# Mixture-of-experts stage: four-block super blocks with stationary weights, streamed rows and a raw-weight ring

## The reference

```python
logits = x @ gate_weight.T                       # 4096 tokens, E = 64 experts
top_val, top_idx = lax.top_k(softmax(logits), 8) # 8 experts for each token
...                                              # secondary picks may be remapped
order = jnp.argsort(flat_e); tok = order // 8
xs = x[tok]                                      # 32768 routed rows, sorted by expert
gu = lax.ragged_dot(xs, swap(gate_up_proj), group_sizes)   # 1024 -> 2 x 384
gate, up = jnp.split(gu, 2, axis=-1)
hact = jax.nn.silu(gate) * up
y = lax.ragged_dot(hact, swap(down_proj), group_sizes)     # 384 -> 1024
out = jnp.zeros_like(x).at[tok].add(y * w[:, None])        # weighted scatter-add
```

## Time and profile before

| what | value |
|---|---|
| runs | 8266.21, 8266.89 and 8268.61 us, median 8266.89 us |
| profiled execution, span from first to last instruction | 8265.9 us |
| PE busy in the span | 7509.6 us, 91% |
| first matmul of the expert stage | 3801.4 us |
| expert stage from there to the end | 4464.5 us, 54% of the span |
| blocks of the expert stage | 287 (64 of them the first of an expert) |

### The profile page before, as it was taken

How to read it: one execution, slowest core, us unless ns; L and a number is a source line. 1 busy time by engine, 2 the same in 40 slices (tenths; PEclk the granted TensorE clock), 3 DMA queues, 4 the chain that set the end, 5 groups by cost and what they waited for, 6 DMA issues and landing times.

```text
span 8265.9 us, 154435 instructions
## 1 busy us (share of the span) xinstructions
PE 7509.6 (91%) x49303; PEld 6709.6 (81%) x49304; DVE 4437.6 (54%) x9784; ACT 3440.3 (42%) x7330; POOL 1747.3 (21%) x1447
## 2 busy tenths in 40 slices
PE   8988998998996899866999999999999999999999
PEld 7877877887885777756888888888888888888888
DVE  6666666666664434455555555555454554555444
ACT  5665665665663212102333333333333333333333
POOL 1111111111110000002222233222222332333222
PEclk9999999999998999978999999999999999999999
DMA  1101101101102221114555555555555555555544
GB/s 56 32 24 49 31 24 49 32 24 49 32 24 75 72 83 61 64 46 119 139 139 137 138 139 138 139 137 138 134 142 126 143 145 126 142 145 139 131 126 115
DMA packets 419950, 786.53 MB, mean 95 GB/s; under 512 B 31120, under 2 KB 295312, under 8 KB 419600
## 3 DMA queue, kind: packets, MB, share of 16 engines
q0 software_dynamic: 89328, 328.81, 18.6%
q1 hardware_dynamic: 330272, 453.35, 16.9%
HBM read 578.60 MB, written 203.46 MB: 95 GB/s over the span
## 4 chain that ended last, share of the span: by engine, by line
PE 38%; issue 7%; POOL 6%; ACT 3%; ACTq 1%; DVE 0%; POOLq 0%; DMA 0%; DVEq 0%
PE ps_gu L1546 8%; PE ps_gu L1548 8%; PE ps_gu L1547 8%; POOL dn_lo L1530 4%; PE ps_y L1546 4%; PE ps_y L1547 3%; PE ps_y L1548 3%; PE ps_xe L1565 2%; ACT gu_hi L1662 2%; PE ps_h L1599 1%; POOL out L1524 1%; ACT y_out L1651 1%; ACTq L1459 1%; ACT xe_hi L1640 0%; DVE at_lo L1726 0%
## 5 line engine op out<-in xcount | busy, mean ns | idle before, releaser
L1546 PE MATMUL ps_gu<-gu_hi,xe_hi 128*128 128x256 f32 x6888 | 1983.3, 288 | 62.5 <-DVE gu_lo L1794 58.2
L1548 PE MATMUL ps_gu<-gu_hi,xe_lo 128*128 128x256 f32 x6888 | 1949.6, 283 | 0.0
L1547 PE MATMUL ps_gu<-gu_lo,xe_hi 128*128 128x256 f32 x6888 | 1949.2, 283 | 0.0
L1546 PEld LDWEIGHTS ps_gu<-gu_hi,xe_hi 128*128 128x128 f32 x6888 | 1323.5, 192 | 115.1 <-DVE gu_lo L1794 85.2
L1547 PEld LDWEIGHTS ps_gu<-gu_lo,xe_hi 128*128 128x128 f32 x6888 | 1321.5, 192 | 7.8
L1548 PEld LDWEIGHTS ps_gu<-gu_hi,xe_lo 128*128 128x128 f32 x6888 | 1320.1, 192 | 0.0
L1805 DVE TENSOR_TENSOR act_h<-ps_gu,silu 128x128 f32<-128x128 f32 x861 | 248.1, 288 | 1824.9 <-ACT silu L1673 1824.9
L1673 ACT ACTIVATE silu<-ps_gu 128x128 f32<-128x128 f32 x861 | 238.9, 277 | 1685.5 <-PE ps_gu L1548 1678.8
L1546 PE MATMUL ps_y<-dn_hi,ht_hi 128*128 128x512 f32 x1722 | 724.2, 421 | 108.5 <-POOL dn_lo L1530 108.5
L345 PE MATMUL ps_qkv<-w_hi,xt_hi 128*128 128x384 f32 x1920 | 708.7, 369 | 52.0 <-DVE v L635 51.9
L1524 POOL DMA_INDIRECT out<-y_out,scatter_i x287 | 516.4, 1799 | 1011.6 <-ACT y_out L1651 974.6
(11 more groups left out here) (273 smaller groups left out, 15357.6 us busy)
## 6 DMA issues: line engine op xcount, KB each, us to landing
gu_raw<-w_gu SPq DMA_DIRECT2D x192, 1024.0 KB, 10.3
dn_raw<-w_down SPq DMA_DIRECT2D x192, 512.0 KB, 4.8
w_raw<-wqkv SPq DMA_DIRECT2D x260, 192.0 KB, 2.6
out<-residual SPq DMA_DIRECT2D x33, 512.0 KB, 2.6
probs<-x SPq DMA_DIRECT2D x32, 512.0 KB, 3.5
attn_out<-out_t POOLq DMA_DIRECT2D x128, 128.0 KB, 2.2
residual<-x SPq DMA_DIRECT2D x32, 512.0 KB, 4.4
stage<-attn_out SPq DMA_DIRECT2D x32, 512.0 KB, 5.2
```

The source lines that it names most:

```text
L1546: pe.matmul(out, a_hi, w_hi, start=first, stop=False)
L1547: pe.matmul(out, a_hi, w_lo, start=False, stop=False)
L1548: return pe.matmul(out, a_lo, w_hi, start=False, stop=last)
```

## The change

An expert now has one unbranched super block of 4 x 128 = 512 rows (`SUP = 4`) and, in an inner loop, tail blocks of 128 rows for what it has beyond 512. With the given inputs these are 64 super blocks and 287 - 256 = 31 tail blocks, since every expert had at least four blocks; where an expert has fewer than 512 rows, the super block is filled up with spare rows of zeros.

In the super block's first layer a 128x128 piece of the weights is stationary and 512 columns of turned rows (`xs_hi`, `xs_lo`) stream; gate and up are products of their own. The result has the hidden features on the partitions, so silu(gate)*up is split in place into `hs_hi`, `hs_lo` without a transpose, and its 128-column slices are the stationary operand of the second layer (`weigh`), whose streamed operand is 512 columns of the down weights as before. Tail blocks are computed as blocks were before. The rows of the next expert's super block are gathered by four indirect transfers and turned between the parts of the second layer. The result of row block i goes to one of two buffers `y_sup[i % 2]`, that of the last one to `y_last`, by way of which tail blocks go too.

Raw weights come in nine chunks of 512 KB through a ring of three slots, with 4 KB in one piece for each partition where there were rows of 1 KB. All six `dn_lo` pieces are POOL's. 512 spare rows of `rows` and `out` are zeroed ahead of `mix_features` instead of 128.

The diff, cut to its core (PE, SP and POOL first, then ACT, then DVE):

```diff
+SUP = 4
+PAD = SUP * P
...
-            sp.dma_start(rows[0:P, 0:H], res[:, 0, :]).then_inc(zero_out, 16)
-            sp.dma_start(rows[0:P, H:H + E], res[:, 0, 0:E]).then_inc(zero_out, 16)
-            sp.dma_start(out[0:P, :], res[:, 0, :]).then_inc(zero_out, 16)
+            for i in range(SUP):
+                a = slice(i * P, (i + 1) * P)
+                sp.dma_start(rows[a, 0:H], res[:, 0, :]).then_inc(zero_out, 16)
+                sp.dma_start(rows[a, H:H + E], res[:, 0, 0:E]).then_inc(zero_out, 16)
+                sp.dma_start(out[a, :], res[:, 0, :]).then_inc(zero_out, 16)
...
-            after(dve.tensor_scalar(blocks[:, :], count[:, :], 1.0, None, ALU.max))
+            after(dve.tensor_scalar(blocks[:, :], count[:, :], float(SUP), 0.0, ALU.subtract, ALU.max))
...
+    HALF = HB * W // 2
+    GUC, CHUNKS = 2 * FB, 3 * FB
+    RING = 3
...
+                t0 = tails_before(eng, e)
+                t1 = tails_before(eng, e + 1)
+                super_block(e, t0, t1)
+                with eng.If(t1 - t0 > 0):
+                    with eng.Fori(t0, t1) as t:
+                        tail_block(e, t)
...
+                if c < GUC:
+                    src = w_gu[e, c // 2, :, c % 2 * HALF:(c % 2 + 1) * HALF]
...
+                    src = w_down[e, (c - GUC) * P:(c - GUC + 1) * P, :]
...
+            def slot_free(e, c):
+                if c < GUC:
+                    sp.wait_ge(lo_ok, START + e * 2 * GUC + 2 * (c + 1))
+                else:
+                    sp.wait_ge(dn_lo_ok, START + e * 2 * FB + 2 * (c - GUC + 1))
...
+                for c in range(RING, CHUNKS):
+                    slot_free(e - 1, c - RING)
+                    load(e - 1, c)
+                for c in range(RING):
+                    slot_free(e - 1, CHUNKS - RING + c)
                     load(e, c)
...
+                pool.wait_ge(ys_ok, START + e * 2 * (SUP - 1) + 2 * i + 2)
+                if i == 0:
+                    pool.wait_ge(ss_ok, START + e + 1)
+                    pool.wait_ge(yl_sent, LOADED + (e + t0 + 1) * 16)
                 stand_alone(pool, passed)
...
+                pool.indirect_dma_start(out, bass.IndirectOffsetOnAxis(ap=scatter_s[:, i:i + 1], axis=0), y_sup[:, i % 2, :], None,
+                                        compute_op=ALU.add).then_inc(ys_sent[i % 2], 16)
...
+            def super_block(e, t0, t1):
+                send_last(e + t0)
+                gather_tail(e + t0)
+                for i in range(SUP):
+                    gather_super(e + 1, i)
+                for n in range(2 * FB):
+                    pool.wait_ge(hi_ok, START + e * 2 * CHUNKS + 2 * GUC + n + 1)
+                    f, a = n // 2, slice(n % 2 * BANK, (n % 2 + 1) * BANK)
+                    pool.tensor_tensor(dn_lo[:, f, a], raw_w[:, f, a], raw(dn_hi[:, f, a]), ALU.subtract).then_inc(dn_lo_ok, 1)
+                for i in range(SUP - 1):
+                    send_super(e, t0, i)
...
+            def turn_super(n, i, tails):
+                pe.wait_ge(rows_s[i], (n + 1) * 16)
+                pe.wait_ge(xt_lo_ok, START + tails * 2)
+                pe.wait_ge(xs_lo_ok, START + n * 2 * SUP + 2 * i)
...
+                    for k in range(HB):
...
+                            pe.wait_ge(lo_ok, START + e * 2 * GUC + 4 * f + k // 2 + 1)
+                        c = slice(k * W + up * P, k * W + up * P + P)
+                        mm = split_product(ps_gu[:, up, :], gu_hi[:, f, c], gu_lo[:, f, c], xs_hi[:, k, :], xs_lo[:, k, :], k == 0, k == HB - 1)
+                    mm.then_inc(up_ok if up else gate_ok, 1)
...
+                    if i == 0:
+                        pe.wait_ge(hs_lo_ok, START + e * FB + f + 1)
+                        pe.wait_ge(dn_lo_ok, START + e * 2 * FB + 2 * f + c + 1)
...
+                    elif f == 0:
+                        pe.wait_ge(ys_ok, START + e * 2 * (SUP - 1) + 2 * (i - 1) + c + 1)
...
+                first_layer(0, 0)
+                first_layer(0, 1)
+                find_rows(e + AHEAD)
+                first_layer(1, 0)
+                first_layer(1, 1)
+                turn_tail(e + t0, e + 1)
+                first_layer(2, 0)
+                first_layer(2, 1)
+                turn_super(e + 1, 0, e + 1 + t0)
+                for f in range(FB - 1):
+                    for c in range(2):
+                        weigh(0, c, f)
+                for c in range(2):
+                    weigh(0, c, FB - 1)
+                for i in range(1, SUP):
+                    turn_super(e + 1, i, e + 1 + t0)
+                    for c in range(2):
+                        for f in range(FB):
+                            weigh(i, c, f)
...
+            def super_block(e, t0, t1):
+                def split(c):
+                    act.wait_ge(raw_in[c % RING], START + (e * 3 + c // RING) * 16 + 16)
+                    if c < GUC:
+                        act.wait_ge(up_ok, START + e * FB)
+                        act.wait_ge(tgu_ok, START + t0 * FB)
+                        dst = gu_hi[:, c // 2, c % 2 * HALF:(c % 2 + 1) * HALF]
...
+                    act.wait_ge(hs_lo_ok, START + e * FB + f)
+                    act.activation(act_s[:, :], ps_gu[:, 0, :], ACT.Silu).then_inc(silu_ok, 1)
...
+                    act.wait_ge(prod_ok, START + e * FB + f + 1)
+                    act.wait_ge(yl_ps, START + (e + t0) * 2 + 2)
+                    act.activation(hs_hi[:, f, :], act_s[:, :], ACT.Copy).then_inc(hs_hi_ok, 1)
...
+                    act.wait_ge(ys_sent[i % 2], LOADED + (e * (2 if i % 2 == 0 else 1) + i // 2) * 16)
+                    for c in range(2):
+                        act.wait_ge(ys_ps, START + e * 2 * (SUP - 1) + 2 * i + c + 1)
+                        a = slice(c * BANK, (c + 1) * BANK)
+                        act.activation(y_sup[:, i % 2, a], ps_y[:, a], ACT.Copy, scale=w_now[:, i:i + 1]).then_inc(ys_ok, 1)
...
+                act.activation(warm[:, :], warm[:, :], ACT.Silu)
+                split(0)
+                split(1)
+                finish_last(e + t0)
+                split(2)
+                split(3)
                 silu_of(0)
-                if first:
-                    split("gu", 2)
+                split_h(0)
+                split(4)
+                split(5)
+                silu_of(1)
+                split_h(1)
+                for c in range(GUC, CHUNKS):
+                    split(c)
+                split_tail(e + t0, t0)
+                silu_of(2)
+                split_h(2)
+                for i in range(SUP):
+                    split_super(e + 1, i)
+                    if i < SUP - 1:
+                        finish(i)
...
+                rest_of(0)
+                rest_of(1)
...
+                gather_tail_index(e + t0, (e + 1) * SUP + t0)
+                gather_super_index(e + 1, t1)
+                rest_of(2)
+                rest_of(3)
...
                 multiply(0)
-                if first:
-                    rest_of(2)
+                rest_of_h(0)
+                rest_of(4)
+                rest_of(5)
+                start_list(after)
+                list_part(after, 0)
+                list_part(after, 1)
+                multiply(1)
+                rest_of_h(1)
+                finish_list(e + AHEAD)
+                keep_tail_weights(e + t0, e)
+                rest_of_tail(e + t0)
+                dve.wait_ge(yl_ok, START + (e + t0) * 2 + 2)
+                dve.wait_ge(wnow_ok, START + e + 1)
+                dve.tensor_copy(w_last[:, :], w_now[:, SUP - 1:SUP]).then_inc(wl_ok, 1)
+                dve.wait_ge(yl_sent, LOADED + (e + t0 + 1) * 16)
+                dve.wait_ge(ss_ok, START + e + 1)
+                dve.tensor_copy(scatter_l[:, :], scatter_s[:, SUP - 1:SUP]).then_inc(sl_ok, 1)
+                multiply(2)
+                rest_of_h(2)
+                for i in range(SUP):
+                    rest_of_super(e + 1, i)
+                    if i == 0:
+                        keep_weights(e + 1)
+                    elif i < SUP - 1:
+                        list_part(after, i + 1)
+                    else:
+                        end_list(after)
...
-        "w_gu": tidy(i["L0_ffn_gate_up_proj"].reshape(E, 2, FB, P, H).transpose(0, 2, 4, 1, 3).reshape(E, FB, H, 2 * P)),
+        "w_gu": tidy(i["L0_ffn_gate_up_proj"].reshape(E, 2, FB, P, HB, P).transpose(0, 2, 5, 4, 1, 3).reshape(E, FB, P, HB * 2 * P)),```

Two places in the order of the instructions. PE, where the first layer of a block goes over into the second, before (`ps_h` takes the transpose of h, `ps_xe` those of the next rows):

```order
L1547 MATMUL ps_gu<-gu_lo,xe_hi 128x256
L1548 MATMUL ps_gu<-gu_hi,xe_lo 128x256
L1596 REGISTER_ALU
L1599 MATMUL ps_h<-ident,act_h 128x128
L1561 ISA
L1563 ISA
L1565 MATMUL ps_xe<-ident,x_rows 128x128 x8
L1596 REGISTER_ALU
L1599 MATMUL ps_h<-ident,act_h 128x128
L1609 REGISTER_ALU
L1546 MATMUL ps_y<-dn_hi,ht_hi 128x512
```

(15 more changed lines are left out.)

482 lines of the change are left out of this document (258 added, 224 removed).

## The result

The changed kernel took 7976.39 us (median of 4 runs, 7973.0 to 7983.38), the kernel before 8266.77 on the same chip: ratio 0.9648, interval 0.9636 to 0.966. That is 290 us less; the forecast was 346. The measured 7976 lies in the likeliest case's own range, 56 us above its number.

A forecast was written before the change was run, and what follows sets the result against it. PE, busy for 91% of 8265.9 us, bounds the kernel. 3821.4 us before the expert stage plus 4099 (super blocks 3597, borders 27, tails 464, end 11) gave 7920 us; range 7865 to 8045.

The forecast's parts named there:

- the likeliest case: Whole kernel: the sum of PE's work and waits holds, 7920 us, own range 7870 to 7980, chance 0.66.
- start: First matmul of the expert stage: at 3821.4 us, from 3801.4 before plus 7 for zeroing and 13 for the opening.
- work: PE's stream in the super blocks: 56.2 us each, 3540.6 us for 63 of them.
- end: Launch's end, last result scaled and scattered: the same 11 us as before; 67.2 with the last super block.
- The border, 0.8 us: Between super blocks of two experts: PE idle 0.8 us as before, under DVE's first remainder; 27 us in all.
- rival 1's third case: Border where ACT's table load comes in full behind DVE's work: 1.3 us; the rival gives 7985 to 8110, chance 0.17.
- Tails, 15.0 us: 31 tail blocks: 15.0 us for each of thirty ahead of a new expert, 14.3 for one, 464 in all.
- The super, 56.2 us: One super block on PE: triples 49.7, five turns of rows 5.2, list 0.99, restarts 0.3; before, four blocks cost 62.0.
- The rule against the row: First-layer matmuls: doubling width saves 0.010 us each, 1.5 us per expert by trace row; skill page gives 0.4 us.
- Waits: Inside a super block: weights, POOL's down remainders (2.2 us slack), last h part (0.5) and result buffers (3.6) stay hidden.
- Zeroing 7, opening 13: Ahead of the expert stage: nine more zeroing transfers cost 7 us, three more turns of rows with gathers 13.
- Rivals 3, 4, 5: Better than the sum, 7840 to 7865, 0.06; late sends, 8430, 0.04; few experts take the super block, excluded by counts.

The follow-up runs named there:

- Experiments 1 and 2: Changed kernel with DVE's value loads behind the first four remainders, 7896.32 us; changed kernel with DVE's list of rows one row block earlier, 7893.99 us.
- experiment 4: Changed kernel with the super block's first layer streaming its 512 columns as two matmuls of 256: 8045.06 us.
- Experiments 5: Kernel before with unused SBUF ahead of the stationary rows, 64 bytes for each partition or a large tile: 8174.04 and 8174.07 us.
- experiment 7: Changed kernel with late value loads, earlier list, tail gather before scatter, zeroing behind weights, plus 192 or 64 unused bytes ahead of xs_hi: 7828.24 and 7884.79 us.
- Experiment 3: Changed kernel with the tail's gather ahead of the scatter on POOL and the zeroing transfers behind the first weights on SP: 7933.48 us.
- experiment 8: Changed kernel with late value loads, earlier list, tail gather before scatter, and twelve zeroing transfers behind the first batch's context loads: 7841.82 us.
- experiment 9: Changed kernel with late value loads, earlier list, tail gather before scatter, zeroing behind context loads, and unused bytes at three places: 7811.03 us.

## Why the prediction was right, and by how much off

The mechanism was right: PE's stream is the bound, and four row blocks in one took out transposes, restarts and the waits inside. 7920 was 56 low. Against the profiled span of 7971.4 the terms were off by +2.7 (start), -56 (work), +73.5 (borders), +28 (tails) and +2.0 (end). That the sum came so near is luck in part: 102 us too few for borders and tails stood against 56 too many for the work of the supers.

- **The border, 0.8 us.** This term failed. I took 1.17 us of issue from the border of before, where only that much stood between DVE's work and its next cast. That issue held the same two value loads; here, behind the list, the first of them takes 1.32 in place of 0.3, and 2.54 us pass. The border was 2.4 us, 53 us more in all, and it brought 20 us of low clock, which the sum did not have. It is rival 1's third case (1.3 us for a late border) at half of the experts. Experiments 1 and 2 show the cause, and the clock's part. The sum had no low clock on either side: the window that it took for an expert of before stood at 1.00, and it did not count the 23 stretches elsewhere in that stage.
- **Tails, 15.0 us.** I took the tail from the last block of an expert before and held that row gathers cost nothing on PE, since they are issued early. That holds for the supers' gathers; I did not walk POOL's queue for the tail's, which stands behind the scatter of the last result: 0.9 us more in each of 31. Experiment 3 takes it out, and then the tail is 14.5, under the 15.0.
- **The super, 56.2 us.** It was 55.32. The medians of a first-layer triple are 0.69 as forecast. A turn of rows costs less than its own 1.04, since the next matmul starts ahead of its end: 0.79 by the starts, and 0.09 more until the one behind it (0.33 in place of 0.23). 5 x (1.04 - 0.88) = 0.8 is nearly the whole difference:

```profile
4190.90 1.04 PE L1632 MATMUL ps_xe<-ident,x_rows 128*128 128x128 f32 x8
4191.69 0.48 PE L1612 MATMUL ps_y<-dn_hi,hs_hi 128*128 128x512 f32 x1
4192.02 0.39 PE L1613 MATMUL ps_y<-dn_lo,hs_hi 128*128 128x512 f32 x1
```

- **The rule against the row.** The row said 0.010 us for each doubled matmul. The Trainium skill ("TensorE: Matmul & The Clock Gate", section "Back-to-back issue gap") gives a fixed part of 2.5 ns, in its formula for an isolated matmul. For the stream of this kernel experiment 4 measured 6 to 8 ns, between the two. Experiments 5 and 7 show that the row of before held a cost of the operands' place: at the offsets that were best for each, two of 256 took 0.228 to 0.234 and one of 512 took 0.227, so between 1 and 7 ns are left for the width. Part of the 1.5 us for each expert that I booked for it is placement. In time the change is worth 290 us against the kernel before as it stands, and some 198 against the same kernel with 64 unused bytes (medians of different chips), while the changed kernel had a place that cost it some 20 (experiment 7).
- **Waits.** PE had no wait on `dn_lo` or `hs_lo`, and none on the result buffers. POOL's remainder of 512 columns took 1.30 us at the mean (2.06 in the earlier trace rows), so its cover was never near its end:

```profile
L1591 POOL TENSOR_TENSOR dn_lo<-raw_w,dn_hi 128x512 fp32r<-128x512 f32 x384 | 485.2, 1298 | 1007.8 <-ACT dn_hi L1793 1007.8
```

- **Zeroing 7, opening 13.** Their sum of 20 was 2.7 short, but its parts do not stand as I had them. The first matmul of the mix stage came 7.4 us later after SP's first transfer than before, and by the stage's last gate matmul only 1.2 of them were left (3646.6 - 2524.5 against 3641.5 - 2520.6). The opening came to 17.6: 14.2 from the first turn of rows to the first matmul, for three turns more, and 3.4 ahead of it, from the last matmul of `route` on, where POOL was busy for 8.49 us in place of 3.72. What is left, 3.8 us, the changed kernel was late before it came to the first edit; the start of the stage differed by up to 12 us among the runs that leave all ahead of the experts as it was. The two windows, before and then after:

```profile
3742.30:3774.60 32.30, 2.12 (x34) 1.73 (x32) 23.33 (x33) 0.00 (x0) 3.72 (x8) 0.50 0.48 164
3774.60:3801.40 26.80, 7.25 (x80) 6.67 (x80) 18.89 (x30) 7.32 (x12) 3.56 (x2) 0.63 0.20 41
```

```profile
3747.40:3783.10 35.70, 2.13 (x35) 1.74 (x33) 23.31 (x35) 0.00 (x0) 8.49 (x15) 0.50 0.20 62
3783.10:3824.10 41.00, 13.13 (x104) 11.39 (x104) 21.99 (x34) 10.32 (x18) 3.75 (x3) 0.54 0.20 52
```

  The reason for 7 was wrong as well: I put it near an issue time of 5.1. The nine more issues alone took 8.2 us (2526.18 to 2534.34), and it is likely the bytes that set this: 3.1 MB at the 0.4 MB/us that the DMA engines moved at most in this stretch are some 7.7 us, and the context loads stand behind the transfers and the wait for them. Experiment 3, which moved them behind the weights and kept them ahead of the context, changed almost nothing, and SP stood for 8 us in the wait for their landing; experiment 8, which moved all twelve behind the context loads, gave 9.4 us at the stage's first matmul. No run changes the number of issues and the bytes apart from each other.
- **Rivals 3, 4, 5.** Not seen. Rival 3's border without a wait wasn't reached by any run: the 0.45 us that stay are ACT's chain.

## What to carry to other kernels

Where the border between two loop rounds is priced, write down the whole queue of each engine there, register reads too: work that hid behind another block's stream is bare once the blocks are merged. Two things ahead of one wait may both seem to be the cause; take out each alone, and if both give the same time, their sum was. Before a width or a tile size is credited with a per-instruction gain, shift the operands by 64 bytes: here that alone, with the low clock that went with it, was worth 95 us, a third of the whole change. And count the stretches at the lower clock over the whole stage, in both kernels: one window of one expert showed none of the 23.

## What the runs showed of the hardware

- The time between matmuls changed with where the operands start in SBUF. With stationary and streamed operand at equal offsets within 256 bytes it was 0.120 us for 256 columns and 0.227 for 512 (0.227 to 0.231 in the second layer); with the offsets 0 and 192 it was 0.114 to 0.118, and 0.226 to 0.234; with 64 and 192 it was 0.119, and 0.232. Why, no run shows. The unused bytes moved all tiles behind them, so a part of other engines' reads and writes in it is not excluded. Three offsets were tried, and that 256 bytes are the right measure is an assumption that two distant places with the same time bear out (experiment 5), while 0.114 and 0.117 at the same offset show that it is not all (experiment 9).
- After 2.3 us without work the granted clock was at its lower level for 3.3 us at 14 of 33 borders, with 0.45 at none. In the kernel before it fell at 23 of 64 first blocks, behind three waits of 0.7 to 1.0 us; with 64 bytes or the large tile ahead of the rows, behind the same waits, at 3 and at 2 (one trace each). What distinguishes these places from the others stays open.
- A register load of DVE from SBUF took 0.31 us at the median of 195. Right behind the last piece of the list it took 1.3 at 32 borders, and with the second load 2.5 passed in all; ACT's took 0.28 at the median.
- POOL's two-input remainder took 2.06 us in the kernel before and 1.30 in the changed one, same shape; that less DVE work ran beside it was not tested by itself.
